# TensorE adds each scanned state behind its other products of a step, not ahead of them

## The reference, cut to what matters

```
x = x + mamba(cond(x))              # layer 0: conditioner, then mixer
x = x + moe(subject_linear(x))      # layer 0: 8 experts, 2 chosen
x = x + attention(lora_ffn(x))      # layer 1
x = x + moe(adapter(x))             # layer 1: 32 experts, 4 chosen

# the mixer's recurrence, for each token t and each of n = 16 states
dA = exp(delta_t * A_n)
h_n = dA * h_n + delta_t * B_t[n] * x_t
y_t = sum_n C_t[n] * h_n + D * x_t
```

## Time and profile before

| | |
|---|---|
| median of 3 runs | 3804.92 us (3804.19 to 3807.61) |
| span of the profiled execution | 3793.6 us |
| device time beyond that span, by the median | 11.3 us |
| TensorE busy | 3438.3 us (91%) |
| VectorE busy | 2286.6 us (60%) |
| ScalarE busy | 1540.0 us (41%) |
| mixer | from about 130 us to 1584 us of the span |

### The profile page before, as it was taken

The page is one execution under the profiler, slowest core; times in us unless marked ns, Lnnn a source line. Parts: engine busy times, 40 slices in busy tenths (PEclk is TensorE's granted clock), DMA queues, the critical chain, the costliest instruction groups (busy, mean ns, idle before and its releaser), DMA issues. The chain is left out here.

```text
span 3793.6 us, 37524 instructions
## 1 busy us (share of the span) xinstructions
PE 3438.3 (91%) x11356; PEld 1798.5 (47%) x11357; DVE 2286.6 (60%) x2808; ACT 1540.0 (41%) x2923; POOL 638.5 (17%) x768
## 2 busy tenths in 40 slices
PE   7798989889898986599979999999999999987996
PEld 4344443434343432266634444444444444445775
DVE  3699999999999999622214353535343444433334
ACT  3555546464646463133314242333333242323443
POOL 0000202020202021223300010110202020205772
PEclk9899999999999998799989999999999999998998
DMA  2122222222222223422130001010101010036557
GB/s 78 56 76 86 80 80 81 79 81 86 81 79 82 83 86 119 151 69 66 61 123 1 26 30 40 16 48 8 55 1 55 1 55 1 32 133 208 158 157 266
DMA packets 157913, 291.45 MB, mean 77 GB/s; under 512 B 27600, under 2 KB 84560, under 8 KB 156624
## 3 DMA queue, kind: packets, MB, share of 16 engines
q1 hardware_dynamic: 129216, 225.01, 18.4%
q0 software_dynamic: 20352, 57.17, 4.1%
q10 hardware_dynamic: 8208, 7.54, 0.6%
HBM read 195.74 MB, written 93.90 MB: 76 GB/s over the span
## 5 line engine op out<-in xcount | busy, mean ns | idle before, releaser
L1206 PE MATMUL ps<-hs,ident 128*128 128x512 f32 x1024 | 515.4, 651 | 123.7 <-DVE hs L1327 123.7
L1321 DVE TENSOR_TENSOR_SCAN hs<-dA,hs 128x2048 f32<-128x2048 f32 x128 | 565.5, 4418 | 7.0 <-DVE hs L1313 0.5
L427 POOL COPY rows<-slot 128x64 f32<-128x64 f32 x48 | 12.1, 282 | 2729.3 <-DVE new_pl L564 2704.2
L1886 PE MATMUL ps<-pT,V 128*128 128x512 f32 x1024 | 450.7, 593 | 0.9 <-DVE pT L2054 0.9
L1271 ACT ACTIVATE dA<-dl,w_An 128x511 f32<-128x511 f32 x512 | 325.9, 709 | 261.0 <-DVE hs L1321 260.5
L1206 PEld LDWEIGHTS ps<-hs,ident 128*128 128x128 f32 x1024 | 209.9, 209 | 412.9 <-issue 257.8
L1313 DVE TENSOR_TENSOR hs<-u,bb 128x2048 f32<-128x2048 f32 x128 | 292.4, 2285 | 20.0 <-PE ps L1206 19.9
L1886 PEld LDWEIGHTS ps<-pT,V 128*128 128x128 f32 x1024 | 189.6, 190 | 221.1 <-issue 214.7
L1327 DVE TENSOR_TENSOR hs<-hs,cb 128x2048 f32<-128x2048 f32 x128 | 290.0, 2266 | 0.0
L1456 POOL DMA_INDIRECT slots<-og,idt x232 | 241.8, 1042 | 260.3 <-DVE og L1544 199.9
L423 POOL DMA_INDIRECT sorted<-rows,new_pl x192 | 274.8, 1431 | 63.6 <-issue 44.8
(11 more groups left out here) (353 smaller groups left out, 5394.6 us busy)
## 6 DMA issues: line engine op xcount, KB each, us to landing
bb<-bcd SPq DMA_DIRECT2D x128, 256.0 KB, 3.5
cb<-bcd SPq DMA_DIRECT2D x128, 256.0 KB, 3.2
xg<-sorted SPq DMA_DIRECT2D x232, 136.0 KB, 2.1
slots<-zeros SPq DMA_DIRECT2D x136, 128.0 KB, 3.2
qrg<-slots SPq DMA_DIRECT2D x32, 512.0 KB, 17.6
W0u<-modd SPq DMA_DIRECT2D x40, 256.0 KB, 3.4
rg<-slots SPq DMA_DIRECT2D x32, 256.0 KB, 4.7
w_Lr<-in_Lora SPq DMA_DIRECT2D x8, 576.0 KB, 3.9
```

Of the source, the lines that this page charges most:

```text
L1206: ins = pe.matmul(ps[:, j, :], ident[:, :], m.hs[:, N % 3, j, :], start=False, stop=(N % NS == NS - 1))
L1321: dve.tensor_tensor_scan(state, m.dA[:, N % 2].rearrange("p j t -> p (j t)"), state, 0.0, ALU.mult, ALU.add).then_inc(s_h, 1)
L1886: ins = pe.matmul(ps[:, 6 + j, :], V[:, m, h * D + j * P:h * D + (j + 1) * P], pT[:, i % 2, h % 2, m, :], start=(h == 0 and m == 0), stop= ...
```

## The change

In steps 1 to 15 of a batch row TensorE issues its other products of the step first and `add_state(N-1)` behind them. In step 0 the add keeps its place, since the skip term starts the next sum in the same banks. Nothing is added or left out; the other engines' lists are the same.

```diff
                         for n in range(NS):
-                            if NS * b + n:
-                                add_state(NS * b + n - 1)
                             if n == 0:
                                 if b:
+                                    add_state(NS * b - 1)
                                     pe.wait_ge(s_y, JI * b)
                                 skip_term()
                                 if b:
...
                                 ahead_pe(pe, n, m, c, kc)
                                 if n == 13:
                                     gate_products(kc)
+                            if n:
+                                add_state(NS * b + n - 1)
                     add_state(last - 1)
```

## The result

The changed kernel takes 4016.88 us (median of 4 runs, 4013.3 to 4021.32) against 3804.56 us: a ratio of 1.0562, with a 95% interval from 1.0549 to 1.0575. It is 212 us slower, where 213 were forecast.

A forecast was written before the change was run, and what follows sets the result against it. VectorE sets the pace in the mixer; the change moves the deadline of TensorE's add. Waits of 171 us plus 42 us for the clock make 213 us, from 3804.9 to 4018 us, 5.6% slower; range 3960 to 4065.

The forecast's parts named there:

- the clock's 2.0: TensorE at a lower clock after idle times in steps 6 to 8: three spells by 2.0 us in seven rows, 42 us.
- 2: State input waits for the late add behind the conditioner's first products: a new wait of 8.80 us.
- 3: The old order's wait at the state input is gone: -2.33 us, all that the change gives.
- 10, 11, 12: TensorE goes on without a gap, 10.3 us a step against VectorE's 8.9: 1.4 us in each step.
- The rule that decides: A state input overwrites a buffer the add three states back must have read; that add now stands last in TensorE's step.
- Rival (c): No change, the three buffers hide it all: 3805 us, 3 in 100.
- (d): Faster: earlier products bring inputs forward, the 19.9 us of waits vanish and no new ones come: 3785 us, 3 in 100.
- (e): Half of it: only the waits of steps 2 and 10 to 12 stay, 64 us: 3870 us, 6 in 100.
- steps 4 and 7 to 9: State inputs wait for adds behind products needing VectorE's late inputs: 2.64, 4.0, 4.0 and 4.3 us without the clock.
- Rival (b): Lower-clock spells longer or more, four of 3.1 us in each row, 87 us: 4063 us, 12 in 100.
- Rival (a): TensorE's clock stays at its upper level: 3976 us, 15 in 100.
- Row 0: First batch row, no output product in front, conditioner starts early, so steps 2 and 3 fall out: 17 us without clock.

The follow-up runs named there:

- the run with the half-filled idle times: Changed kernel plus 9, 3 and 6 products by zero in TensorE's idle times of steps 6, 7 and 8: 3985.8 us, ratio 1.0474 to the kernel before.
- the tails: Kernel before, with the add behind the products in steps 3, 6, 7 and 8 alone: 3979.5 us, ratio 1.0473.
- all but step 1: Changed kernel with step 1's add left ahead of the products: 4035.6 us, ratio 1.0612 to the kernel before.

## Why the prediction was right

The forecast was 4018 us, the measured median is 4016.88. Term by term, for batch row 2:

| step | predicted, without clock | with the clock's 2.0 | measured |
|---|---|---|---|
| 2 | +8.80 | | +8.81 |
| 3 | -2.33 | | -2.33 |
| 4 | +2.64 | | +3.99 |
| 7 | +4.0 | +6.0 | +5.56 |
| 8 | +4.0 | +6.0 | +5.63 |
| 9 | +4.3 | +6.3 | +5.86 |
| 10, 11, 12 | 1.4 each | | 1.28, 1.28, 1.76 |
| gate | 0 | | -1.04 |
| sum | 25.6 | 31.6 | 30.8 |

From gate to gate the row grew by 215.02 - 183.70 = 31.3 us; 0.5 us of it stand at no wait of these. The gate's term is the clock's too: the row's last add took 5.40 us before and takes 3.70 now.

The rule that decides is shown and not only argued: the waits stand at the state input, in the steps named, and a fourth buffer removes them with the order unchanged. Rival (c), that three buffers hide it all, and (d), that the kernel gets faster, fail with that. So does (e): the waits of steps 4 and 7 to 9 are there. Rival (b), four spells of 3.1 us, had their number right for rows 2 to 6 and their size wrong. Of the signs that the prediction named, two are off: its waits of "some 210 us" at the state input are 240.5, where its own sum (19.9 + 213) makes 233, and the longest, in step 2 of row 1, is 10.5 us and not near 9, behind a skip term of 5.40 us.

**Sizes that were off.** The clock took 1.3 us in step 4, which I had not counted among the spells, and 1.6 and not 2.0 in each of the other three. Rival (a) is out by the run with the half-filled idle times. By the rows, the waits of steps 4 and 7 to 9 stand above their terms without the clock by 10.8 us in row 0, 6.7 in row 1 and 6.1 in each of the other five full rows, together some 48 us (an estimate) where 42 were forecast. The half-filled run gives back some 30 of it.

The Trainium skill (TensorE: Matmul & The Clock Gate, Part 1: The HAM clock gate) has "the ramp penalty is <1% of a typical kernel span". It says so of the slow matmuls with which a kernel starts; the prediction took it as a ceiling of 38 us for spells in the middle, which that sentence does not give. As such a ceiling it would not have held here: 48 us are 1.2% of 4017.

Row 0 was taken at 17 us and 6 for the clock. Its gate moved from 313.74 to 345.10 us, 31.4 us. Its first products of step 1 now wait for ScalarE, and start at the lower clock:

```profile
141.39 3.64 PE L390 MATMUL ps<-x,w_Wn 128*64 128x512 f32 x4 [11.12 <-ACT sz L1295]
```

Before, an add stood there and took the slow start. The step of the prediction that says the conditioner of row 0 "can start long before the first `out`, so steps 2 and 3 fall out" failed: the state input of its step 2 waits 2.79 us. Those of steps 7 to 9 wait 8.0, 6.5 and 7.1 us, more than in a full row, at a mean clock of 0.87 in the row: the clock's term of 6 us was too small here. Row 0 is 8 us more than forecast. Rows 1 to 6 grew by 186.1 us together (gate to gate from 313.74 to 1419.48 before, from 345.10 to 1636.93 after) against 6 by 31.6 = 189.6. In all the last full row's gate moved by 217.5 us where 213 were forecast. Behind the last gate of the mixer another 3.6 us went, which the prediction had at nothing (1571.77 us to the end of the span before, 1789.08 after).

That the median then matches within 2 us is luck in part. The span grew by 220.9 us and the median by 212.3. The term of 11.3 us for what lies around the span was no constant: after, the profiled execution took 4016.36 us with a span of 4014.5, so that 1.9 us lie around it. With as much around it, the profiled execution of before took some 3795.5 us (an estimate) and was a faster one than its median of 3804.9. Row 0 (8 us too little) and what follows the mixer (3.6) are balanced by rows 1 to 6 (3.5 too much) and by these 9.

**What the sum hid.** It counts the waits in a row one after another. As an account of this kernel it holds. It is no list of prices: the late add in step 1 alone costs 40 us and its removal from the changed kernel saves nothing. The wait in step 2 is paid for out of TensorE's own chain from the skip term on. The expectations for the tails and for all but step 1 took the terms as separable, and their times were missed by 27 us and by 33 and 58 us. In the tails' run the loss is 33 us above the expected one (180 for 147), and the waits put 38 more at step 4 and 4 less at steps 7 to 9. So it is TensorE's chain with the wait for ScalarE in it, and not the clock. What stays open is what sets the clock at the skip term, 3.70 us in one order and 5.40 in another.

## What to carry to other kernels

Where a ring of buffers ties two engines, moving the reader's release behind its other work takes away as much slack as that work is long, even if no work is added: ask what the last input of that work is, how long the reader's tail behind it is, and how long the writer needs from that input to the next reuse. Here the tail was 10.4 us against 6.4, and one more buffer made the order indifferent.

A short wait may hide another. Two attempts to remove one of 2.33 us found another behind it at the next buffer pair, the traces: of 2.35 us with a fourth buffer, of 3.4 with an add sooner. And waits taken from one profile add up for that profile only; undone one by one they are not additive.

## What the runs showed of the hardware

A TensorE that waits can pay twice: in row 2 of the changed kernel the products behind idle times of 9.1, 3.5 and 6.5 us took 1.6 to 1.7 us longer, at the lower clock (1.2 GHz) for part of them, and the engine waiting for them lost as much. The length of the idle time straight ahead does not tell alone whether this happens. In the same row the turning products lost 1.3 us behind an idle time of 1.97 us, and an add behind one of 3.45 us lost nothing:

```profile
773.06 3.70 PE L1206 MATMUL ps<-hs,ident 128*128 128x512 f32 x8 [3.45 <-DVE hs L1328]
```

Products by zero in the idle time brought the three groups back to full speed, and the changed kernel gained some 30 us by 18 such products in each batch row; 4.9 us a row were gained there and 1.6 lost again in the rest of the row, above all behind a skip term that had turned slow. And the filling costs at once where it is longer than the idle time: with 18, 6 and 12 products in place of 9, 3 and 6 the gain of some 30 us became a loss of 47.
